# Start of a four-layer attention kernel: the taps' DMA behind the weights, a semaphore for each half of x, earlier clearing on GpSimd, a fused shift, warming products regrouped

## The reference

```python
def _L0_conv_ref(x, gamma, beta, wq, bq, wk, bk, wv, bv, wp, bp):
    hn = group_norm(x, 32 groups of 4 channels, eps=1e-6) * gamma + beta
    q = wq @ hn + bq; k = wk @ hn + bk; v = wv @ hn + bv
    attn = softmax(q.T @ k * c ** -0.5)
    return wp @ (v @ attn.T) + bp + x
# then: attention over positions and channels; an 8-head attention; a linear
# attention block with 3x3 depthwise convolutions and a feed-forward part
```

## Time and profile before

| | before |
|---|---|
| median of 3 runs | 95.25 us |
| the three runs | 93.95, 95.25, 97.65 us |
| span of the profiled execution | 94.5 us, of 1637 instructions |
| PE busy, PEld busy | 84.6 us (90%), 61.4 us (65%) |
| DVE, ACT, POOL busy | 67.1, 53.2, 30.9 us |
| q0 product of batch 0 starts (L909) | 9.55 us |

### The profile page before, as it was taken

One profiled execution on the slowest core, in us unless ns is written; L12 is line 12 of the kernel. 1 busy time (PEld: TensorE's weight loads), 2 busy tenths in 40 slices (PEclk: granted clock), 3 DMA queues, 4 the chain that ended last, 5 costly groups with the idle time before them and its releaser, 6 DMA issues.

```text
span 94.5 us, 1637 instructions
## 1 busy us (share of the span) xinstructions
PE 84.6 (90%) x510; PEld 61.4 (65%) x510; DVE 67.1 (71%) x195; ACT 53.2 (56%) x168; POOL 30.9 (33%) x62
## 2 busy tenths in 40 slices
PE   4987999999999789899999999899999868979960
PEld 1333789756776569588776766678899635756540
DVE  1527456684677675997778699697999983877861
ACT  3200035924942504899989996996199454903830
POOL 7006199200000009910010003048876840235320
PEclk9999999999999999999999999999999999999999
DMA  1899100000000000772930000000000000000003
GB/s 52 228 363 390 44 0 0 0 0 7 0 0 3 0 0 0 237 210 68 285 98 0 0 0 0 0 7 0 0 0 3 0 0 10 0 0 3 0 0 111
DMA packets 5561, 5.01 MB, mean 53 GB/s; under 512 B 304, under 2 KB 5040, under 8 KB 5552
## 3 DMA queue, kind: packets, MB, share of 16 engines
q1 hardware_dynamic: 5264, 4.18, 13.4%
q10 hardware_dynamic: 288, 0.72, 2.6%
HBM read 3.59 MB, written 1.31 MB: 52 GB/s over the span
## 4 chain that ended last, share of the span: by engine, by line
PE 51%; DVE 19%; ACT 9%; issue 6%; POOL 6%; DMA 5%; SPq 0%; POOLq 0%; DVEq 0%; ACTq 0%
PE bank L886 7%; PE bank L1067 6%; DMA wa<-in_pack_a 5%; POOL vacc L277 3%; PE bank L1086 3%; ACT p L400 3%; DVE st L506 3%; PE bank L879 3%; PE bank L909 2%; DVE nmax L700 2%; PE bank L1004 2%; PE bank L926 2%; PE bank L981 2%; PE bank L1147 2%; PE bank L1034 2%
## 5 line engine op out<-in xcount | busy, mean ns | idle before, releaser
L367 ACT ACTIVATE p<-bank,nmax 128x256 f32<-128x256 f32 x32 | 14.9, 487 | 1.2 <-DVE nmax L700 0.9
L277 POOL TENSOR_TENSOR vacc<-vacc,p 128x240 f32<-128x240 f32 (+1 forms) x16 | 10.8, 675 | 6.8 <-ACT p L400 5.1
L886 PE MATMUL bank<-wa,p 128*128 128x128 f32 x80 | 12.5, 275 | 0.3 <-ACT pT L374 0.3
L700 DVE TENSOR_REDUCE nmax<-bank 128x2 f32<-128x512 f32 x16 | 10.7, 681 | 2.6 <-PE bank L1067 2.6
L236 POOL TENSOR_TENSOR rs<-ve,mhalf 128x2 f32<-128x2 f32 x8 | 5.6, 695 | 17.7 <-DVE ve L513 17.7
L894 PE MATMUL bank<-warm 128*128 128x512 bf16 x28 | 10.1, 495 | 1.2 <-DVE warm L519 1.2
L886 PEld LDWEIGHTS bank<-wa,p 128*128 128x128 f32 x80 | 9.3, 140 | 2.6 <-issue 0.9
L257 POOL TENSOR_SCALAR qh<-q,wb 128x256 f32<-128x256 f32 x8 | 4.5, 585 | 18.4 <-DVE q L687 18.4
L1147 PE MATMUL bank<-convw,fsh 128*128 128x128 f32 x72 | 9.0, 275 | 0.0
L1147 PEld LDWEIGHTS bank<-convw,fsh 128*128 128x128 f32 x72 | 8.7, 192 | 0.2
L1067 PE MATMUL bank<-k,qh 128*128 128x256 f32 x32 | 8.2, 383 | 0.4 <-ACT p L367 0.4
(11 more groups left out here) (205 smaller groups left out, 179.3 us busy)
## 6 DMA issues: line engine op xcount, KB each, us to landing
wc<-in_pack_c SPq DMA_DIRECT2D x1, 649.0 KB, 8.6
wb<-in_pack_b SPq DMA_DIRECT2D x1, 612.0 KB, 7.5
tapw<-in_taps ACTq DMA_DIRECT2D x1, 576.0 KB, 6.7
stack_q<-stacks_q SPq DMA_DIRECT2D x2, 256.0 KB, 3.2
stack_k<-stacks_k SPq DMA_DIRECT2D x2, 256.0 KB, 3.8
stacks_q<-parts_q SPq DMA_DIRECT2D x2, 192.0 KB, 2.1
stacks_k<-parts_k SPq DMA_DIRECT2D x2, 192.0 KB, 2.3
wa<-in_pack_a SPq DMA_DIRECT2D x1, 320.0 KB, 6.5
```

Of the source, the lines that this page charges most:

```text
L277: nc.gpsimd.tensor_add(vacc[b][:, oy, ox], vacc[b][:, oy, ox], vprod[n - 1][:, iy, ix]).then_inc(s["vsum_d"], 1)
L367: nc.scalar.activation(p2[u % P2_RING][:, t, :], tiles(bank[u % S2_BANKS])[:, t, :], ACT.Exp, bias=nmax2[b][:, h, t:t + 1], accum_out=sum2 ...
L700: nc.vector.tensor_reduce(nmax2[b][:, h, :], tiles(bank[u % S2_BANKS]), AX.X, ALU.max, negate=True).then_inc(s["max2_d"], 1)
L886: last = nc.tensor.transpose(tiles(dst)[:, i, t * 128:(t + 1) * 128], src[:, t, i * 128:(i + 1) * 128], ident)
```

## The change

Five edits, all in the first 10 us of the program.

1. The DMA of `tapw` is issued by SP after `pack_c`, not by ACT after x of batch 1.
2. x of batch 0 and x of batch 1 have a semaphore each, and the statistics of each batch wait for its own.
3. GpSimd clears `v2` before it waits for the variance, not after the power.
4. `ma0` goes. The shift is made by one fused instruction for each batch, and `hn0` of a batch waits for its own shift.
5. TensorE makes 8 and 3 warming products where it made 9 and 4, and 2 more behind L905, ahead of the q product.

```diff
         def _(sp):
-            sp.dma_start(x0[0][:, :], x[0].rearrange("c h w -> c (h w)")).then_inc(s["x_in"], 16)
+            sp.dma_start(x0[0][:, :], x[0].rearrange("c h w -> c (h w)")).then_inc(s["x0_in"], 16)
...
             sp.dma_start(wc[:, :], pack_c).then_inc(s["c_in"], 16)
+            sp.dma_start(tapw[:, :], taps.partition_broadcast(128)).then_inc(s["tap_in"], 16)
...
                     nc.gpsimd.memset(fsh[dx][b][:, :, :], 0.0).then_inc(s["zeroed"], 1)
+            for b in range(NB):
+                nc.gpsimd.memset(v2[b][:, :, :], 0.0).then_inc(s["v2_zeroed"], 1)
...
-            inverse_root(rstd0[:, :], ve0[:, :], s["ve0_d"], s["rstd0_d"], 0, NB)
-            for b in range(NB):
-                nc.gpsimd.memset(v2[b][:, :, :], 0.0).then_inc(s["v2_zeroed"], 1)
+            pool.wait_ge(s["ve0_d"], 1)
+            nc.gpsimd.tensor_tensor(rstd0[:, :], ve0[:, :], mhalf[:, 0:NB], ALU.pow).then_inc(s["rstd0_d"], 1)
...
-            act.dma_start(x0[1][:, :], x[1].rearrange("c h w -> c (h w)")).then_inc(s["x_in"], 16)
-            act.dma_start(tapw[:, :], taps.partition_broadcast(128)).then_inc(s["tap_in"], 16)
+            act.dma_start(x0[1][:, :], x[1].rearrange("c h w -> c (h w)")).then_inc(s["x1_in"], 16)
...
-                dve.wait_ge(s["x_in"], 32)
+                dve.wait_ge(s[f"x{b}_in"], 16)
...
-            nc.vector.tensor_mul(ma0[:, :], a0[:, :], gs0[:, :, 0]).then_inc(s["vec"], 1)
-            vec_done("ma0")
-            dve.wait_ge(s["vec"], vec_at("ma0", 1))
-            nc.vector.tensor_scalar(nb0[:, :], ma0[:, :], A("beta"), None, ALU.subtract).then_inc(s["vec"], 1)
-            vec_done("b0")
-            dve.wait_ge(s["vec"], vec_at("b0", 1))
             for b in range(NB):
+                nc.vector.scalar_tensor_tensor(nb0[:, b:b + 1], a0[:, b:b + 1], gs0[:, b, 0:1], A("beta"),
+                                               ALU.mult, ALU.subtract).then_inc(s["vec"], 1)
+                vec_done("nb0")
+            for b in range(NB):
+                dve.wait_ge(s["vec"], vec_at("nb0", b + 1))
...
-            keep_clock(9, bank[7])
+            keep_clock(8, bank[7])
...
-            keep_clock(4, bank[7])
+            keep_clock(3, bank[7])
             pe.wait_ge(s["a2_in"], 16)
...
+            keep_clock(2, bank[7])
```

More of the change, by code:

```diff
@@ L97, in build @@
         gs0 = sb("gs0", [128, NB, 2])
-        nm0, ve0, rstd0, a0, ma0, nb0 = (sb(name, [128, NB]) for name in ("nm0", "ve0", "rstd0", "a0", "ma0", "nb0"))
+        nm0, ve0, rstd0, a0, nb0 = (sb(name, [128, NB]) for name in ("nm0", "ve0", "rstd0", "a0", "nb0"))
         hn0 = per_batch("hn0", [128, N])
@@ L180, in shifted @@
                     (slice(max(0, dy), H + min(0, dy)), slice(max(0, dx), W + min(0, dx))))
-        NAMES = """a2_in warm_set vec a_in x_in b_in c_in tap_in zeroed mhalf_set wg_done conv_w wpv_p wpv_w bias0_w gbv_w outw_c w1g_w w1c_w
+        NAMES = """a2_in warm_set vec a_in x0_in x1_in b_in c_in tap_in zeroed mhalf_set wg_done conv_w wpv_p wpv_w bias0_w gbv_w outw_c w1g_w w1c_w
             w2g_w w1m_p w2m_p w2c_w gin0_d g0_p ve0_d rstd0_d hn0_d q0_p k0_p v0_p q0_d k0_d v0_d s0_p max0_d e0_d
```

## The result

The changed kernel takes 92.6 us, the median of 20 executions (92.12 to 94.13), against 96.16 us for the kernel before, again of 20 (93.34 to 98.89). By all executions that is 3.7% less. The comparison that counts leaves out the executions that lie more than 1.5% above the fastest of their kernel, and gives a ratio of 0.986, 95% interval 0.9835 to 0.9883: 1.4% faster. I had forecast 91.3 against 95.25, 4.2% faster. That 3.7% and 1.4% differ is the subject of this case: TensorE's clock stood low for longer in most executions of the kernel before, as the experiments show.

The account below looks back on a forecast made before the run. The chain to q0, waiting for `pack_a`'s first part, and q and k products at the lower clock were taken as the bound. From 94.5 us, 1.7 at q0 and 2.0 for the clock gave 90.8; 0.5 added made 91.3, range 90.0 to 94.0.

Parts of the forecast that it names:

- The clock term: TensorE from q0 to v: products at 2.4 instead of 1.2 GHz, 3.44 us instead of 5.56, gain 2.0 us.
- The reason for an early step: TensorE before q0: no gap over about 0.1 us from 1.19 on, so 2.4 GHz is reached by 7.85.
- The signs of being wrong: L909 still at 634 ns, L904 still waiting for the DMA, or a longer distance from q0 to the end.
- The reading of the scatter: Three-run median 0.75 us above the profiled span, partly from the moment of the clock's step; 0.5 added to 90.8.
- The average, gain 0.9: Group average ahead of q0: starts at 4.7 instead of 5.61 once its weights land by 3.9; bounds 0 and 1.0.
- Why the transfers were slow: Start of loading: 590 KB of taps move beside `pack_a`'s first part, 177 GB/s at 3.0 to 4.5 us, later 410.
- rival 3: `pack_a`: slow stretch belongs to any DMA start, parts land as now, new warming products delay q0 0.4 us; 94.9, chance 0.06.
- Clearing early, 0.7: Scale L543 on VectorE: held until GpSimd's second memset ended; without it 0.23 instead of 0.93 us, gain 0.7.
- The meeting of `convw` with L598: `convw` on POOL at about 11.4 to 15.2, L598 at 15.6; if they met, one step of 0.45 us lost.
- Rival 1: Clock steps up later, halfway through q and k or at their end: 92.1, median about 92.8; chance 0.17.
- Rival 2: Clock's step stays at 13.7 us, v at 14.35, gain only 0.8: 93.7, median 94.4; chance 0.10.
- rival 4: Gain lost again in a later stage by a falling clock or a new POOL and DVE meeting: 93 to 95; chance 0.07.

Follow-up runs that it names:

- no_warm_mid: The changed kernel without the 3 and the 2 warming products between the group average and q0 (8 stay); median 94.55 us over six executions, none clean.
- before_again: The kernel before, with no edit, run and profiled once more; median 95.02 us over six executions, ratio to itself 0.980.
- the matched pair: Second profiles of the unedited kernel before and the unedited changed kernel, clock stepping at 6.6 and 6.9 us; spans 91.8 and 91.0 us.
- clear_late: The changed kernel with `v2` cleared behind the power on GpSimd again, as before; median 94.21 us over six executions, clean ones 93.09 and 93.25.
- shift_unfused: The changed kernel with the shift again as two dependent instructions, `ma0` and `nb0`; median 92.81 us over six executions, clean ones 92.54 to 92.91.
- taps_on_act: The changed kernel with the `tapw` DMA back on ACT behind x of batch 1; median 96.48 us over twelve executions, the one clean 94.91.
- warm_9_4: The changed kernel with 9 and 4 warming products again and none behind L905; median 92.68 us, all six executions clean, 92.55 to 92.74.
- taps_only: The kernel before with only the `tapw` DMA moved behind `pack_c` on SP; median 93.68 us over six executions, clean ones 93.27 to 93.71.
- warm_only: The kernel before with only the warming products regrouped to 8, 3 and 2; median 95.77 us over six executions, none clean.

## Why the prediction was wrong

- **The clock term, and what it was a difference from.** This is the step that failed: "So the clock gives 2.0 to 2.1; I take 2.0." The size is right for the pair that I had: the products from q0 to v took 3.56 us instead of 5.56, and no_warm_mid prices a late step at 2.2. But I took one profiled execution with a late step for the kernel. before_again steps at 6.6 us without any edit and has its v 3.56 behind q0. Where the comparison goes by undisturbed executions of both, this term is zero, and the matched pair gives 1.1 at q0 and 0.8 in the span where my sum had 3.7. By all executions the medians are 3.6 apart, but that this is near 3.7 is partly luck: of 39 executions of the kernel before, 29 had a mean clock under 0.99, that is a half-level stretch behind the first step, which my sum did not have; at most six lost by the late step alone, as it had it.
- **The reason for an early step.** I took the step to follow from work without a gap: "it has stepped to 2.4 GHz by 7.85, after 6.6 us of work without a gap". Two executions of the changed kernel, with the same eight products first, stepped at 4.0 and at 6.9; the three products behind the average ran at the upper level in one and at the lower in the other:

```profile
L894 PE MATMUL bank<-warm x3: 376/377/377, 4.8 to 5.3; 128*128 128x512 bf16 x3
L894 PE MATMUL bank<-warm x3: 587/634/634, 5.2 to 6.0; 128*128 128x512 bf16 x3
```

  TensorE then stood idle for 0.8 us before q0 in the first, where I had allowed 0.1, and the level stayed. no_warm_mid, whose TensorE stood idle for 1.16 us before the first of the folding products and for 0.29 before q0, stepped only at 13.1. What sets the moment of the step stays open.
- **The signs of being wrong.** None of the three that I had named appeared in the changed kernel's profile. They all looked at the kernel after, and the error was in what I took the kernel before to be.
- **The reading of the scatter.** "Part of that must be the moment of the clock's step" was right, and should have led further: a spread of 93.95 to 97.65 in three runs said that a clock that costs 2 us in one run may cost nothing in another. And the 0.75 of which I added 0.5 compared a time with a span. About 1.8 us lie around every span, so the profiled execution was a bad one, not a good one. The span of 90.8 that I forecast is the span measured; 91.3 for its time was 1.3 too low.
- **The average, gain 0.9.** 0.98 against the first profile, 0.25 against before_again, where nine warming products held TensorE to 5.00. The landing of the first part of `pack_a` scatters from 4.8 to 6.8 us with the taps beside it, and I had one draw. My value for its landing without them (3.9) was right, if at the late end: 3.56 to 3.95 in ten profiles. The second part landed at 5.5 to 7.1 where I had 4.7 to 5.8; L904 waited 0.94 us for it in clear_late and 0.42 in shift_unfused, but `hn0` came later still.
- **Why the transfers were slow.** I blamed the taps for the slow stretch. It stayed without them; the busy time of the changed kernel by stretch reads

```profile
3.00:4.50 1.50, 1.49 (x5) 0.32 (x3) 1.23 (x6) 0.00 (x0) 0.40 (x1) 1.00 0.90 193
6.00:9.00 3.00, 2.21 (x12) 1.56 (x12) 1.97 (x8) 0.38 (x1) 0.43 (x1) 1.00 0.98 389
```

  193 GB/s at 0.90 busy, as the earlier trace rows with 177 at 0.77. From 3.0 to 4.5 us the ten profiles with the taps on SP have 192 to 234 GB/s, the four others 177 to 328. So the early stretch is slow in either order, as rival 3 supposed. Nor do the bytes explain the landing: to 6.83 us taps_on_act moved 192 GB/s, 1311 KB, where both halves of x, the first part and all taps are 926. Transfers queued behind the first part had thus moved before it had landed in full. Why it lands later beside the taps, and why so unevenly, stays open.
- **Clearing early, 0.7.** Right: 0.69 between the scales of the matched pair, 0.5 to 0.7 in clear_late.
- **Shift, 0.1.** 0.19 in the pair, about 0.2 in shift_unfused's median.
- **Semaphores, zero.** Too low by about 0.1.
- **Warming products.** q0 waits for `hn0` in every profile of a clean execution but that of taps_on_act, so the two behind L905 cost nothing. The grouping is worth about 0.1, not the steadiness of the clock: warm_9_4 is as steady.
- **The meeting of `convw` with L598, "inside the range".** It happened in the two profiles of the changed kernel, 0.74 and 0.65 us instead of 0.43, and gave back 0.2 to 0.3.
- **Rival 1**, a later step, belonged to the wrong kernel: 35 of 39 executions of the kernel before were not clean. The fall over the q and k products is seen in the profiles of taps_only and warm_only; where the 29 executions of the kernel before with a lower mean had theirs, no trace shows. **Rival 2** did not come. **Rival 3** was right that the slow stretch belongs to the start and not to the taps, and wrong that the transfers would therefore not move: taps_on_act and the ten profiles with the taps on SP refute it. In the Trainium skill, "DMA: Bandwidth & Descriptors", "Queues, rings and completion order" has each DMA engine take turns between the queues for which it has work. The landings agree with that, 4.8 to 6.8 us with the taps in the other queue and 3.56 to 3.95 without; the turns themselves are shown by no run here. Of **rival 4** one piece came, the fall in layer two, in at most 2 of 20 executions.

## What to carry to other kernels

When runs of one kernel spread by more than the effect that is sought, find out from the trace at which clock level the profiled execution ran, and say for each term of the sum whether it is a difference between kernels or between executions. Small transfers on which a chain waits belong ahead of large ones in every queue, also the other engine's. Clearing on GpSimd belongs where VectorE waits anyway, and the gaps of TensorE ahead of its first dense work are worth filling, since here they decided the rate of that work: without the five products between, no execution of six was clean.

## What the hardware showed that I had not expected

- The granted clock does not only step up late: it fell to 0.50 for 3.4 us at 8.8 us (taps_only) and 9.0 us (warm_only) of the span, after TensorE had been busy for 1.52 of 3.0 and 1.13 of 3.2 us, and at 21.1 us in the changed kernel after TensorE had been busy for 3.0 of 3.0 us.
- The same transfer of 72.5 KB, second in its queue behind x of batch 0, landed at 4.8, 4.9, 5.6 and 6.8 us from run to run with 590 KB in the other queue, and between 3.56 and 3.95 in ten profiles without.
- A two-column tensor_scalar on VectorE took 0.92 us beside a GpSimd memset that only writes (five profiles), and 0.23 otherwise (nine).
- A VectorE tensor_tensor of 128x256 (L598) and a GpSimd one of 128x128 (`convw`), both with two inputs in SBUF, hold each other up, and the later one waits: 0.74 instead of 0.43 us for VectorE's when both started at 15.24, 0.68 instead of 0.46 for GpSimd's when VectorE's had started 0.06 us before.
